# A new order of scores, transposes, products and projections in the attention stage of a four-stage transformer kernel

## What is computed

```python
# B, S, H = 8, 1024, 256
x = L0_attn_x
n = layernorm(x)
q, k, v = n @ Wq.T, n @ Wk.T, n @ Wv.T
scores = q @ k.T / sqrt(H)              # per batch, 1024 x 1024
scores = where(causal, scores, -inf)
x = x + softmax(scores, axis=-1) @ v
# ... then the three other stages, unchanged
```

## Time and profile before

| | us |
|---|---|
| median of 3 runs | 2576.71 |
| lowest, highest | 2575.89, 2580.19 |
| profiled execution, own time | 2576.54 |
| its span in the profile | 2574.8 |
| attention stage, first to last product of `w7` in the last batch | 0 to about 433 |

### The profile page before, as it was taken

How to read it: one execution, slowest core, us unless ns; L and a number is a source line. 1 busy time by engine, 2 the same in 40 slices (tenths; PEclk the granted TensorE clock), 3 DMA queues, 4 the chain that set the end, 5 groups by cost and what they waited for, 6 DMA issues and landing times. The chain is left out here.

```text
span 2574.8 us, 43725 instructions
## 1 busy us (share of the span) xinstructions
PE 2368.8 (92%) x16024; PEld 2185.2 (85%) x16024; DVE 1779.7 (69%) x3293; ACT 1294.5 (50%) x2026; POOL 704.8 (27%) x468
## 2 busy tenths in 40 slices
PE   6888987699999988999999999998999998499999
PEld 6887887699999976988988988987999998499998
DVE  5666565799999966575565575565678784877774
ACT  4444443443443424564564564454667664355555
POOL 1011001345445433123123123122344431211110
PEclk9999998799999998999999999987999999799999
DMA  5000000000000000000000000011000010000000
GB/s 177 0 0 0 0 0 1 20 1 0 0 0 0 1 1 17 9 8 16 12 4 16 12 4 16 12 46 42 17 25 16 24 41 1 35 26 25 24 24 33
DMA packets 42971, 45.69 MB, mean 18 GB/s; under 512 B 3088, under 2 KB 41872, under 8 KB 42640
## 3 DMA queue, kind: packets, MB, share of 16 engines
q1 hardware_dynamic: 42896, 44.69, 5.3%
HBM read 27.90 MB, written 16.78 MB: 17 GB/s over the span
## 5 line engine op out<-in xcount | busy, mean ns | idle before, releaser
L1877 DVE TENSOR_TENSOR m_a_lo<-m_a,m_a_hi 128x512 fp32r<-128x512 f32 x128 | 124.2, 986 | 90.8 <-ACT m_a_hi L1836 90.8
L1832 ACT ACTIVATE d_a<-d_ps_wide,d_b,d_w_gain 128x512 f32<-128x512 f32 x128 | 100.1, 782 | 136.6 <-PE d_ps_wide L272 134.4
L1287 POOL TENSOR_TENSOR p_kf<-p_kf,p_k_shift 128x1024 f32<-128x1024 f32 x64 | 119.5, 1904 | 155.4 <-DVE p_k_shift L1422 155.4
L1789 PE MATMUL m_ps_z<-m_w_hi,m_a_hi 128*128 128x256 f32 x512 | 146.2, 286 | 0.0
L1789 PE MATMUL d_ps_z<-d_w_hi,d_a_hi 128*128 128x256 f32 x512 | 143.6, 280 | 1.0 <-DVE d_a_lo L1877 1.0
L1789 PE MATMUL m_ps_z<-m_w_hi,m_a_lo 128*128 128x256 f32 x512 | 144.2, 282 | 0.0
L1789 PE MATMUL m_ps_z<-m_w_lo,m_a_hi 128*128 128x256 f32 x512 | 144.1, 281 | 0.0
L1789 PE MATMUL d_ps_z<-d_w_lo,d_a_hi 128*128 128x256 f32 x512 | 143.4, 280 | 0.0
L1789 PE MATMUL d_ps_z<-d_w_hi,d_a_lo 128*128 128x256 f32 x512 | 142.6, 278 | 0.0
L1877 DVE TENSOR_TENSOR d_a_lo<-d_a,d_a_hi 128x512 fp32r<-128x512 f32 x128 | 85.7, 689 | 76.3 <-ACT d_a_hi L1836 71.9
L1832 ACT ACTIVATE m_a<-m_ps_wide,m_b 128x512 f32<-128x512 f32 x128 | 87.9, 687 | 87.9 <-PE m_ps_wide L272 87.6
(11 more groups left out here) (356 smaller groups left out, 8524.5 us busy)
## 6 DMA issues: line engine op xcount, KB each, us to landing
residual<-in_x SPq DMA_DIRECT2D x8, 1024.0 KB, 11.8
attn<-p_attn SPq DMA_DIRECT2D x32, 256.0 KB, 2.2
m_attn<-attn SPq DMA_DIRECT2D x16, 512.0 KB, 3.8
out<-residual SPq DMA_DIRECT2D x16, 512.0 KB, 2.9
raw_weights<-in_d_q SPq DMA_DIRECT2D x2, 1024.0 KB, 7.2
d_scale<-in_d_scale SPq DMA_DIRECT2D x2, 1024.0 KB, 5.8
raw_weights<-in_m_w1T SPq DMA_DIRECT2D x1, 1024.0 KB, 4.9
raw_weights<-in_m_w2T SPq DMA_DIRECT2D x1, 1024.0 KB, 8.0
```

Source lines behind the costliest of these rows:

```text
L1287: pool.tensor_tensor(f, f, k_shift[:, i, :].unsqueeze(2).broadcast_to([P, HEADS, M]), ALU.subtract).then_inc(k_shifted, 1)
L1789: mm = pe.matmul(z, a, w[:, f, :], start=(f == 0 and k == 0 and j % 2 == 0), stop=(f == FC - 1 and k == 2), skip_group_check=True)
L1832: act.activation(self.a[f % RING][:, :], self.ps_wide[f % 2][:, :], self.func, bias=self.b1[:, f:f + 1], scale=gain(f))
L1877: dve.tensor_tensor(self.a2[1][:, f, :], self.a[f % RING][:, :], self.a2[0][:, f, :].bitcast(F32), ALU.subtract).then_inc(self.a_lo, 1)
```

## The change

The order in which the steps stand in a batch changes, and ACT gets an order of its own. Per batch, PE and DVE before (n of the next batch included):

`s2 t0 n0 | s3 w0 t1 n1 | s4 w1 t2 n2 | s5 w2 t3 w3 t4 n3 n4 | s6 w4 t5 n5 n6 | s7 t6 w5 | X0 X1 t7 w6 X2 X3 w7 | p0 ... p7 s0 s1`

(in the kernel a tile's own steps stand before its n pieces), and after:

`s2 s3 t0 t1 n0 s4 w0 w1 n1 t2 t3 s5 w2 w3 n2 t4 s6 w4 t5 n3 n4 s7 t6 w5 n5 n6 | X0 X1 w6 t7 p0 p1 w7 X2 X3 | p2 ... p7 s0 s1`

ACT has no share in w, n0, n1 or n2; its list puts `t2` before `s4` and `t3` before `s5`. The pieces beside the projections are counted from p2 on, not from p0: the scale after p2, the moments after p3 to p6, their combination after p7, the rounding after s1. In the last batch the tail is w6, t7, w7 where it was t7, w6, w7. No instruction is added or taken away.

```diff
-        AHEAD = ["", "", "n0", "n1", "n2", "n3 n4", "n5 n6", ""]
-        TILES = ["", "", "s2 t0", "s3 w0 t1", "s4 w1 t2", "s5 w2 t3 w3 t4", "s6 w4 t5", "s7 t6 w5"]
+        ORDER = "s2 s3 t0 t1 n0 s4 w0 w1 n1 t2 t3 s5 w2 w3 n2 t4 s6 w4 t5 n3 n4 s7 t6 w5 n5 n6"
+
+        ORDER_OF_SCALAR = "s2 s3 t0 t1 t2 s4 t3 s5 t4 s6 t5 n3 n4 s7 t6 n5 n6"
...
-        def schedule(tile, front, skip_turn):
-
-            def projections(b, beside):
-                for m in range(len(FILLS)):
+        def schedule(tile, front, skip_turn, order=ORDER):
+
+            def projections(b, begin, beside):
+                for m in range(begin, len(FILLS)):
                     front(b, "p", m)
-                    beside(m)
-                tile(b, "scores", 0)
-                tile(b, "scores", 1)
+                    beside(m - 2)
+                for i in range(2):
+                    tile(b, "scores", i)
+                    beside(len(FILLS) - 2 + i)
...
-                for i in range(2, TB):
-                    for e in TILES[i].split():
+                for e in order.split():
+                    if e[0] in STEPS:
                         tile(b, STEPS[e[0]], int(e[1:]))
-                    ahead(*AHEAD[i].split())
+                    else:
+                        ahead(e)
                 ahead("t0", "t1")
+                tile(b, "weigh", TB - 2)
                 tile(b, "turn", TB - 1)
-                tile(b, "weigh", TB - 2)
+                ahead("p0", "p1")
+                tile(b, "weigh", TB - 1)
                 ahead("t2", "t3")
-                tile(b, "weigh", TB - 1)
                 if last:
                     for m in range(len(FILLS)):
                         beside(m)
                 else:
-                    projections(b + 1, beside)
+                    projections(b + 1, 2, beside)
...
-                projections(0, lambda m: None)
+                projections(0, 0, lambda m: None)
...
-            schedule(tile, front, lambda eng: skip_uses(eng, turned_hi))(act)
+            schedule(tile, front, lambda eng: skip_uses(eng, turned_hi), ORDER_OF_SCALAR)(act)
```

## The result

| | before | after |
|---|---|---|
| median us (4 runs each) | 2576.98 | 2537.40 |
| lowest, highest | 2575.89, 2580.19 | 2533.56, 2540.59 |
| profiled execution, own time | 2576.54 | 2533.56 |
| first transpose of the next stage | 442.41 | 403.97 |

The ratio is 0.9844, 95% interval 0.9826 to 0.9861: 39.6 us less. The prediction was 34 less (2542.5), range 2533 to 2556.

A forecast was written before the change was run, and what follows sets the result against it. PE, busy 92%, was taken as the bound, its waits mostly for DVE's low parts. Gains 24.4 + 7.7 - 2.3 = 29.8, with the clock 34.1, took 2576.5 us to 2542.5; range 2533 to 2556.

The forecast's parts named there:

- S to E: From PE's start on s0 to its end of s7: waits before t0, w1, w3 go, w2's grows; gain 2.95 us per batch.
- the replay: The new list laid out on PE, DVE and ACT from s0's start, with durations from the old kernel's profile rows.
- the extra 0.8 for the first and the last batch: Attention stage: about 0.4 us more gain in the first batch (no combination or rounding), 0.4 in the last (no n0, n1).
- E to S: From s7's end to the next batch's s0: t7's wait goes, X0's stays; gain 1.1 us in each of seven passages, 7.7.
- The tail of the last batch: Last batch, without X and p: w6 and w7 wait 1.5 and 1.8 us for low parts; cost 2.3 us.
- The clock: Attention stage: three of four falls of PE's clock to half speed go, about 1.4 us each; gain 4.3 us.
- all falls gone and DVE a little earlier at w2: Rival, 15%: attention stage gains 1.4 us more from the clock and 8 x 0.5 at w2; 2534 to 2540 us.
- the 2540 to 2545 that had 51%: The forecast's own band for the whole kernel's time in us, given the remaining chance, 51%, after the rivals.
- the wait only moves to w2: Rival, 8%: w2 waits 3 to 4.5 us, the gain from s0 to s7 shrinks to nothing; 2565 to 2571 us.
- the clock falls as often as now: Rival, 20%: falls continue after the longer wait before w2, so the 4.3 us are lost; 2545 to 2550 us.
- The ring through ACT's exponential of tile 4: Slower rival, 3%: PE waits for w0, ACT for t2, DVE for tile 4; extra turns at w0 and w2, 2587 us.
- The later stages: Sign for stages behind attention: the prediction is wrong if they change by more than 2 us.

The follow-up runs named there:

- e7_wait2: The new kernel with six more moment instructions on VectorE (2.0 us) right ahead of t2's low part: period 48.82 against 46.87, 2562.84 us.
- e5_dveorder: The new kernel with VectorE's own order (n0 behind t3, n1 and n2 behind t4) and last-batch tail t7, w6, w7: period 45.33, 2521.49 us.
- e3_oneorder: The new kernel with ScalarE in the same order as the other engines: period 46.88 against 46.87, 2541.49 us in one run.
- e1_front: The new order only up to w5, with the old kernel's tail and pieces beside the projections: period 48.49, 2546.84 us, 0.9886 of the old kernel.
- e11_t7_first: The new kernel with t7 ahead of w6 again, p0 and p1 still ahead of w7: period 48.85 against 46.87, 2551.93 us.
- e10_p_behind_w7: The new kernel with p0 and p1 behind w7, X2 and X3 again, w6 still ahead of t7: period 48.71 against 46.87, 2552.92 us.
- e4_lasttail: The new kernel with the last batch alone ending t7, w6, w7 as before the change: period 46.88, 2531.53 us in one run.
- e2_tail: The old order up to w5 on all engines, with only the new tail: period 50.95 against 51.30, 2576.05 us, 0.9999 of the old kernel.

## Why the prediction was right, point by point

- *S to E, 2.95 per batch.* It was 3.15 (26.65 - 23.50). The waits before t0, w1, w3 are gone, the one before w2 is 1.35 drawn, 1.5 by my reckoning, and made by DVE's list: e7_wait2 adds to it one for one, e5_dveorder takes it away, e3_oneorder shows that ACT has no part in it. The waits themselves are as forecast, 1.5 before w2 and 0.18 before w0 (0.17 in the replay). The forecast is too small by 0.2 because PE's own work is not the same in the new order: 21.8 instead of 22.0, when the two waits are taken off. Steps of one kind now stand together: w2 and w3 take 2.61 in a row where they took 1.18 and 1.54, s3 takes 1.50 behind s2 where it took 1.56 behind t0. Of the extra 0.8 for the first and the last batch only the last batch's half came, which shows no wait before w2; in the first it is still 1.23.
- *E to S, 1.1 per batch.* It was 1.30 (24.65 - 23.35), and X0's wait stayed at 0.85 drawn. The 0.2 are mostly inside t7, which takes 0.79 instead of 1.01 (I had given it a tenth), and inside X0 and X1 (0.94 instead of 1.02). The reading was too narrow as well: I put the gain down as the old wait of 1.05 that goes. In the new order that wait would have been 1.79 (1.63 drawn, e1_front, e11_t7_first), and w7 would have waited 1.7 as well (e10_p_behind_w7). The two moves are worth 1.84 and 1.98 and pay for what the first half of the change makes late. The replay of the whole list had both covers in it, and so the total holds, but the two halves do not add up (3.16 against 4.43).
- *The tail of the last batch, 2.3.* 2.27 in e4_lasttail.
- *The clock, 4.3 for three of four falls.* All four are gone. The two in the middle of the stage cost 1.46 and 1.58 (periods of 52.76 and 52.88 against 51.30), so at 1.5 each, an estimate from these two, the four cost 6.0. This is the term that was mis-sized most. The stage's gain of 38.4 is then about 25.7 from S to E (24.4 forecast), 8.9 from E to S (7.7), less 2.3, plus 6.0 of clock (4.3); that makes up the 4.3 by which it exceeds my 34.1. The Trainium skill ("TensorE: Matmul & The Clock Gate", Part 1: The HAM clock gate) says that activity releases the throttled state, and the prediction read from it that all four would go, as they did. It is no rule for any denser list, though: e1_front is denser by 2.8 us a batch and has three falls.
- *The rivals.* The median, 2537.40, lies in the band of a rival (2534 to 2540, 15%: all falls gone and DVE a little earlier at w2) and not in the 2540 to 2545 that had 51%. Its first half is what happened; its second did not, since t2's low part starts at 11.92 as in the replay, and the shorter steps named above, 0.4 a batch, stood in its place. That the wait only moves to w2 is out (it moved, but as 1.5 and not 3 to 4.5). That the clock falls as often as now is out in this kernel, though not for longer waits (e7_wait2). The ring through ACT's exponential of tile 4 is out by e3_oneorder: taking it apart changes nothing.
- *The later stages.* I wrote that the prediction was wrong if they changed by more than 2 us. They were 4.5 shorter in the profiled execution, so by that sign the prediction was wrong, and over all profiled executions they lie between 2126.4 and 2135.3, with no part in the change. The bound was too strict; one profiled execution could not show how far they vary. The stage's own 38.4 would have put the median at 2538.6, so the range was not met by that luck.

## What to carry to other kernels

When engines walk a common list in order, a wait is ended by putting independent work between a producer's chain and its consumer; count the chain link by link on each engine, for the new list as a whole, because a half of a reordering can be worth next to nothing alone (0.35 of 4.43 here). The engine whose list has no gap ahead of the wait is the one to relieve next: here moving 2.6 us of VectorE work that nobody was waiting for gave 1.5 us per batch. Judge such an edit by the period of its own loop, since stages behind it may differ by several us from run to run.

## What the runs showed of the hardware

Falls of TensorE's granted clock from 1.00 to 0.50 came in or right behind waits, and the more often the longer PE had stood still. With single drawn waits of up to 1.6 us there was none in the stage, in any kernel. With 2.3 us before w3, and 0.5 before w2 about 4 us earlier, there was one in six of sixteen batches (before, e2_tail); with 0.85 and 0.89 within 3 us of each other in one of seven batches (before); with 0.85 and 1.63 within 3 us in six of fourteen (e1_front, e11_t7_first); with 3.3 us in six of seven (e7_wait2). A fall cost 1.4 to 1.6 us in the kernel before and about 2.4 in most of the batches of e7_wait2. So a wait of 3.3 us costs nearer 6 than 3.3. These are counts from one profiled execution of each kernel.

From its first to its last product of `p_v` by `p_kf`, the unchanged linear-attention stage took 696, 699, 701 or 704.5 us in 13 profiled executions, with three, four, four and six falls of the clock. Kernels whose attention stage was alike (after and e3_oneorder, 0.4 us apart) had either end of it.
